# Causal attention core on one core: scores and row maxima in two 64-row tiles of the TensorE array, from two float32r parts, with the causal mask added by products

## What is computed

```python
q = _rope(q, cos, sin)
k = _rope(k, cos, sin)
k = jnp.repeat(k, Q_PER_KV, axis=2)      # 4 query heads share a key head
v = jnp.repeat(v, Q_PER_KV, axis=2)
scores = jnp.einsum('bqhd,bkhd->bhqk', q, k) * SM_SCALE
scores = jnp.where(mask[None, None], scores, jnp.finfo(scores.dtype).min)
probs = jax.nn.softmax(scores, axis=-1)
ctx = jnp.einsum('bhqk,bkhd->bqhd', probs, v).reshape(B, S, HIDDEN)
out = jnp.einsum('bsh,oh->bso', ctx, w_dense) + b_dense
```

## Time and profile before

| what | us |
|---|---|
| time, median of 3 runs (1273.64 to 1277.37) | 1274.57 |
| the profiled execution | 1276.3 |
| its span in the trace | 1274.5 |
| core block: from the projection's last DVE instruction to the first maxima product | 8.77 |
| core block: maxima of group 0 | 29.01 |
| group 0 | 31.10 |
| groups 1 to 6, each | 31.45 |
| group 7 | 28.80 |

### The profile page before, as it was taken

How to read it: one execution, slowest core, us unless ns; L and a number is a source line. 1 busy time by engine, 2 the same in 40 slices (tenths; PEclk the granted TensorE clock), 3 DMA queues, 4 the chain that set the end, 5 groups by cost and what they waited for, 6 DMA issues and landing times. The chain is left out here.

```text
span 1274.5 us, 21579 instructions
## 1 busy us (share of the span) xinstructions
PE 1097.4 (86%) x5654; PEld 717.9 (56%) x5655; DVE 905.9 (71%) x1775; ACT 704.8 (55%) x1218; POOL 566.7 (44%) x582
## 2 busy tenths in 40 slices
PE   4969999999194899999997787999999947878597
PEld 3847777777182233333333675677777735467454
DVE  5869888887575888888860666888888847444632
ACT  3238787887143177777775131787888824424142
POOL 4335666664556244443331225566666545140200
PEclk9979999999596599999998888999999977989889
DMA  9367899764615550000000183789995561000001
GB/s 351 114 220 185 218 243 286 174 114 60 192 50 155 104 99 19 1 1 1 1 1 1 63 309 111 236 196 258 275 222 103 83 156 67 1 1 1 0 1 66
DMA packets 62798, 151.01 MB, mean 118 GB/s; under 512 B 12224, under 2 KB 17024, under 8 KB 58240
## 3 DMA queue, kind: packets, MB, share of 16 engines
q1 hardware_dynamic: 37440, 95.17, 22.3%
q0 software_dynamic: 22592, 50.27, 20.3%
q10 hardware_dynamic: 2688, 4.65, 1.1%
HBM read 104.89 MB, written 44.97 MB: 118 GB/s over the span
## 5 line engine op out<-in xcount | busy, mean ns | idle before, releaser
L811 POOL DMA_INDIRECT moe_acc_rows<-xn,moe_token_of x94 | 208.0, 2213 | 146.3 <-ACT xn L886 131.1
L923 DVE TENSOR_TENSOR moe_w_lo<-moe_raw,moe_w_hi 128x1536 fp32r<-128x1536 f32 x94 | 165.4, 1759 | 62.9 <-ACT moe_w_hi L874 62.7
L1977 ACT ACTIVATE causal_prob<-causal_sc 128x512 f32<-128x512 f32 (+3 forms) x384 | 166.8, 492 | 70.3 <-PE causal_sc L1882 69.7
L874 ACT CAST moe_w_hi<-moe_raw 128x1536 fp32r x94 | 138.7, 1475 | 78.0 <-issue 76.4
L1864 PE MATMUL causal_mx<-ks,causal_qs 96*128 (+4 forms) x384 | 131.4, 353 | 23.0 <-DMA causal_qs<-causal_parts 16.5
L831 PE MATMUL moe_gu<-moe_w_hi,xt_hi 128*128 128x512 f32 x282 | 148.4, 526 | 0.6 <-DVE moe_w_lo L923 0.6
L1882 PE MATMUL causal_sc<-causal_qs,ks 99*128 (+3 forms) x384 | 120.2, 333 | 1.9 <-ACT causal_prob L1977 1.7
L831 PE MATMUL moe_gu<-moe_w_hi,xt_lo 128*128 128x512 f32 x282 | 111.8, 396 | 0.0
L831 PE MATMUL moe_gu<-moe_w_lo,xt_hi 128*128 128x512 f32 x282 | 110.9, 393 | 0.0
L826 PE MATMUL moe_gu<-moe_raw,xn 128*128 x188 | 98.0, 603 | 5.0 <-ACT moe_w_hi L874 5.0
L1808 POOL TENSOR_SCALAR_AFFINE_SELECT causal_prob<-causal_prob 128x512 f32<-128x512 f32 x64 | 40.9, 639 | 115.9 <-ACT causal_prob L1977 115.5
(11 more groups left out here) (317 smaller groups left out, 2724.5 us busy)
## 6 DMA issues: line engine op xcount, KB each, us to landing
moe_raw<-in_w_gu SPq DMA_DIRECT2D x34, 1024.0 KB, 6.1
moe_raw<-in_w_down SPq DMA_DIRECT2D x34, 512.0 KB, 8.2
causal_qs<-causal_parts SPq DMA_DIRECT2D x45, 128.0 KB, 3.6
moe_acc_rows<-moe_zeros SPq DMA_DIRECT2D x2, 2304.0 KB, 14.7
moe_acc_rows<-x SPq DMA_DIRECT2D x18, 256.0 KB, 2.0
moe_xn_rows<-xn SPq DMA_DIRECT2D x2, 2048.0 KB, 10.7
x<-moe_acc_rows SPq DMA_DIRECT2D x16, 256.0 KB, 6.8
xn<-moe_acc_rows ACTq DMA_DIRECT2D x16, 256.0 KB, 7.2
```

Of the source, the lines that this page charges most:

```text
L811: pool.indirect_dma_start(acc_rows[a], bass.IndirectOffsetOnAxis(ap=token_of[:, b - 3:b - 2].bitcast(U32), axis=0), out_rows[(b - 3) % OUT ...
L874: nc.scalar.copy(w_hi[1 - s][:, :, :], raw[:, bass.ds(at + SPLIT_AT, GU_COLS - SPLIT_AT)].rearrange("p (k n) -> p k n", k=SPLIT)).then_inc ...
L923: nc.vector.tensor_tensor(w_lo[1 - s][:, :, :], raw[:, bass.ds(at + SPLIT_AT, GU_COLS - SPLIT_AT)].rearrange("p (k n) -> p k n", k=SPLIT), ...
L1977: nc.scalar.activation(prob[u % 2][:, h, o:CH], sc[(u * QPK + h) % BANKS][:, o:CH], ACT.Exp, scale=SCALE).then_inc(exp_done, 1)
```

## The change

- The parts are two float32r numbers instead of three bfloat16 ones. ACT casts the first, POOL subtracts the second; ACT's second cast and DVE's `third` are gone. DRAM holds 2 parts of 4 bytes.
- A stack is 3 products of 16 rows. There are two copies of it: rows 0 to 49 for scores (with 2 rows for the maxima), rows 64 to 111 for maxima. A score product and a maximum product thus lie in different halves of the array.
- A diagonal maximum is followed by two bfloat16 products of rows 64 to 127, 128 and 64 columns wide, that add the mask: identity by `later`, in two halves of 64 rows.
- DVE reads all maxima with TENSOR_REDUCE; one more instruction per group (`later_best`) joins the two halves for the later 512 queries.
- `split_maxima` has 3 POOL instructions, `put_maxima` 2 DMAs. `turn_maxima` transposes float32.
- Keys and queries have two slots (g % 2) instead of all groups. The loads for group 0, and those of the maxima of group 1, are issued in the projection block. In the core block SP loads the scores' stack of g + 1 and the maxima's of g + 2, after waits on `neg_in[1]`, `sc_done` and `mx_done`.
- At the start of the projection block ACT issues two more loads (64 x 2 x 128 each), waits for both, and casts `mask_q` and `mask_k`; the cast of `ident_half` is gone.
- In group 7, from step 1 on, scores use 112 rows (`ALL_ROWS`); POOL zeroes rows 64 to 127 of a key slot for it at the group's start (`upper_zero`).
- PE's loop over groups is written out.

```diff
-    Q_PART = (0, 0, 1, 0, 1, 2)
-    K_PART = (0, 1, 0, 2, 1, 0)
-    STACK = len(Q_PART) * HD
-    MROWS = 3
+    Q_PART = (0, 0, 1)
+    K_PART = (0, 1, 0)
+    MROWS = 2
+    MAX_AT = 2 * HD
+    SCORE_ROWS = slice(0, 3 * HD + MROWS)
+    MAXIMA_ROWS = slice(64, 64 + 3 * HD)
+    MASK_ROWS = slice(64, P)
+    ALL_ROWS = slice(0, 64 + 3 * HD)
+    IN_SCORES = (0, HD, 2 * HD + MROWS)
+    IN_MAXIMA = (64, 64 + HD, 64 + 2 * HD)
...
                         if r == KEYS[-1] + 1:
...
-                            for a in range(len(Q_PART)):
-                                sp.dma_start(ks[a * HD:(a + 1) * HD, 0:S], parts_dram[K_PART[a], 0:HD, :]).then_inc(stack_in, 16)
+                            load_keys(sp, IN_MAXIMA, 0, for_maxima_in)
+                            load_keys(sp, IN_SCORES, 0, for_scores_in)
+                        if r == QUERIES[-1] + 1:
...
+                            load_queries(sp, IN_MAXIMA, 0, for_maxima_in)
+                        if r == len(TURN) - 1:
+                            load_queries(sp, IN_SCORES, 0, for_scores_in)
+                            sp.wait_ge(for_maxima_in, 16 * LOADS)
+                            load_keys(sp, IN_MAXIMA, 1, for_maxima_in)
+                            load_queries(sp, IN_MAXIMA, 1, for_maxima_in)
...
+                    for n, what in enumerate(("identity", "later")):
+                        act.dma_start(mask_raw[MASK_ROWS, n, :, :], m.dram[what].rearrange("(a p) k -> p a k", a=2)).then_inc(mask_in, 16)
                     act.wait_ge(swap_in, 16)
                     nc.scalar.copy(swap[:, :], swap_raw[:, :]).then_inc(swap_done, 1)
-                    nc.scalar.copy(ident[:, :], m.ident[:, :]).then_inc(consts, 1)
+                    act.wait_ge(mask_in, 32)
+                    nc.scalar.copy(mask_q[MASK_ROWS, :, :], mask_raw[MASK_ROWS, 0, :, :]).then_inc(mask_ready, 1)
+                    nc.scalar.copy(mask_k[MASK_ROWS, :, :], mask_raw[MASK_ROWS, 1, :, :]).then_inc(mask_ready, 1)
...
-                    for a in range(0, len(Q_PART), 2):
-                        first_queries(sp, a)
...
+                    sp.wait_ge(ones_done, 3)
+                    for g in range(KV - 1):
+                        sp.wait_ge(neg_in[1], 16 * MROWS * (g + 1))
+                        if g:
+                            sp.wait_ge(sc_done, g * NS * QPK)
+                        load(IN_SCORES, g + 1, for_scores_in)
...
+                        if g + 2 < KV:
+                            sp.wait_ge(mx_done, (g + 1) * NMU)
+                            load(IN_MAXIMA, g + 2, for_maxima_in)
...
-                        nc.tensor.matmul(mx[i % BANKS][:, 0:w], qs[0:STACK, bass.ds(at, P)],
-                                         ks[0:STACK, bass.ds(gn * S + kc * CH, w)], start=True, stop=True).then_inc(mx_done, 1)
+                        last = nc.tensor.matmul(mx[i % BANKS][:, 0:w], q_r[MAXIMA_ROWS, at:at + P], k_r[MAXIMA_ROWS, key:key + w],
+                                                start=True, stop=not diagonal)
+                        if diagonal:
+                            nc.tensor.matmul(mx[i % BANKS][:, w - P:w], mask_q[MASK_ROWS, 0, :], mask_k[MASK_ROWS, 0, :], start=False, stop=False)
+                            last = nc.tensor.matmul(mx[i % BANKS][:, w - P // 2:w], mask_q[MASK_ROWS, 1, :],
+                                                    mask_k[MASK_ROWS, 1, P // 2:P], start=False, stop=True)
+                        last.then_inc(mx_done, 1)
...
-                        nc.tensor.matmul(sc[b][:, o:CH], ks[0:STACK + MROWS, bass.ds(g * S + kb * P, P)],
-                                         qs[0:STACK + MROWS, bass.ds(g * QG + (h * S + c * CH + o), CH - o)],
+                        rows = ALL_ROWS if g == KV - 1 and u else SCORE_ROWS
+                        if g == KV - 1 and u == 1 and h == 0:
+                            pe.wait_ge(upper_zero, 1)
+                        nc.tensor.matmul(sc[b][:, o:CH], k_r[rows, key:key + P], q_r[rows, at + o:at + CH],
                                          start=True, stop=True).then_inc(sc_done, 1)
...
-                        nc.vector.tensor_tensor_reduce(found, found, no_later[:, CH - w:CH], 1.0, least, ALU.add, ALU.max,
-                                                       top[:, t, h:h + 1]).then_inc(mx_read, 1)
+                        nc.vector.tensor_reduce(top[:, kc, t, h:h + 1], mx[i % BANKS][:, 0:w], AX.X, ALU.max).then_inc(mx_read, 1)
```

197 lines of the change are left out of this document (94 added, 103 removed).

## The result

The changed kernel is slower: 1315.72 us, the median of four executions (1298.91 to 1334.95), against 1275.14 for four of the kernel before, 3.2% more. The ratio is 1.027, 95% interval 1.017 to 1.037; executions over 1.5% above the fastest of their kernel count as slow and stay out of the ratios, here that of 1334.95, in experiment 6 one of 1491.0 at a mean clock of 0.724. I had forecast 1261 and a range of 1250 to 1272. Its four executions lie 36 us apart, where those of before lie within 4 us, and they go with TensorE's mean granted clock: 0.912, 0.900, 0.896 and 0.882 for 1298.91, 1313.13, 1318.31 and 1334.95. The profiled execution is the last of these, 58.7 us over the profiled execution of before (spans of 1333.1 and 1274.5).

A forecast was written before the change was run, and what follows sets the result against it. PE, DVE and the diagonal steps' chain were taken as close limits, plus mutual waiting. Terms -9.5, -5.7, -0.5, +1.6 and +0.3 gave -13.8: 1262.5 us from the profiled 1276.3, 1261 against the median; range 1250 to 1272.

The forecast's parts named there:

- The step that failed is 5: Middle groups: lighter PE and DVE save 1.35 us a group, 9.5 us over seven, bounds 0 and 18.
- step 7: Maxima of group 0, at granted clock 0.50: 0.5 us won, between 3 lost and 2 won.
- the chain keeps the groups as they are: Rival, groups: fourth score, exponential and mask set all steps, PE's relief only makes PE wait; 1270.5 us, chance 11%.
- Steps 1 to 4: Groups: full pair about 0.23 us, diagonal masks 0.9 more on PE, DVE about 25.5, POOL about 1 us less per half-group.
- step 3: DVE in a group: fused maximum 0.65 us, plain one about 0.60; busy time from 27.04 to about 25.5.
- Step 6: Edge of projection and core blocks: early query loads start the first maximum 5.7 us sooner, bounds 4 and 7.
- Step 8: Start of the projection: two more loads and a cast on ACT lose 1.6 us, from 0.3 to 3.
- Step 9: Group 7: a memset ahead of POOL's first split loses 0.3 us.
- The two slowest rivals: Maxima tile: each product pays its own weight load, 1291 us, 11%; score and maximum tiles don't stream together, near 1300, 3%.

The follow-up runs named there:

- experiment 6: Kernel before with diagonal masks as one full-height bfloat16 product and plain maxima, without the two tiles and float32r: 1280.98 us, ratio 1.0036.
- Experiments 1 and 2: First: kernel before, score and maximum products half as high, 1434.94 us. Second: changed kernel, group 7's scores reading 50 rows instead of 112, executions 1306.43 to 1339.98 us.
- experiment 10: Changed kernel with ACT's mask casts moved to the projection's end and SP's wait and loads for group 1 into the core block: 1312.96 us, one execution.
- experiment 3: Changed kernel without the two mask products of each diagonal maximum: 1296.70 us, ratio 1.016.
- experiment 5: Changed kernel plus 96 unread float32r products, 512 wide, reading rows 0 to 47 only: 1306.62 us, ratio 1.026.
- experiment 4: Changed kernel plus 96 unread float32r products, 512 wide and 128 rows high: 1318.41 us, ratio 1.033.

## Why the prediction was wrong

**The step that failed is 5**, the middle group. I put 30.1 us against 31.45, and the bounds at 0 and 18 won in all. It was wrong in two ways.

The larger one is missing from the prediction: that the clock in the groups might not stay at 1.00. I read 1.00 for groups of full-height products and carried it to products half as high. I weighed the clock only for group 0's maxima (step 7), where it stood at 0.50 already. Experiments 1 and 2 show that half-height products let it fall with PE fully busy. In the profiled execution the seven groups take 53.6 us more; at full clock they would take 7 x (32.48 - 31.42) = 7.4 more, and the other 46 are the clock. In the execution near the median (experiment 10) they take 36.1 more, and 28 are the clock.

The smaller one is the size at full clock: +1.1 a group instead of -1.35. By its parts: tiles and masks together 32.48; without masks 31.07, so the tiles alone win 0.35 where I gave PE 3.4; the masks, which I put at 0.9 of PE's time, cost the group 1.4 in the half-height tile (experiment 3) and 0.7 at full height with plain maxima (experiment 6). PE's busy time, which I had fall by 1.9, rose from 30.1 to 31.6. That a middle group is held by its chain (score, exponential, mask, values), as the rival "the chain keeps the groups as they are" said, fits this, but no run shortens the chain. I had given that rival 11% and taken the middle between two bounds instead of asking who waits for PE in the steps that count.

**Steps 1 to 4** held in most of their single prices. Pairs 0.23 apart: measured 0.23, but 0.33 for the first pair after a change of tile. The 0.6 that I added for such turning had no row behind it. DVE 25.5: 25.45. POOL 1 us lighter a half-group: 12.0 against 13.9 a group. A diagonal unit of 512 columns I put at 0.39; at full clock they follow each other every 0.42 where they stream, and in the diagonal steps mostly every 0.60, at DVE's pace (its plain maximum, 0.60 by step 3). On the rule of the Trainium skill that I weighed there ("TensorE: Matmul & The Clock Gate", Part 3, weight loads overlapping only across row groups) the 0.42 speaks against bare weights on all three products, as my did.

**Step 6**, the edge: 5.7 forecast, 1.9 measured (64.91 against 66.85 us from the first `hi_tile` to the first maximum). The core block starts at 410.28, past the 406 that I had named as a sign of being wrong. I took SP's last issue for what is late next and left out what SP waits for behind it, the landing of writes that are queued behind the loads I had moved. POOL's memsets took 6.2 (0.94 + 3.50 + 1.80), as put.

**Step 7**: 0.5 won forecast, 3.5 lost measured (32.53 against 29.01). The mechanism was in the text with both sizes; the clock stayed at 0.50, a unit costs 0.76 against my 0.75, and PE leads DVE. I chose the wrong branch.

**Step 8**: 1.6 forecast, 4.0 measured, over my bound of 3. The second mask load landed 2.2 us behind the swap cast, the casts took 0.7, and the swap matrix itself landed 10.4 after its issue instead of 9.2.

**Step 9**: 0.3 forecast, 2.3 measured. The clock of 0.94 is not all of it: in experiment 5 group 7 ran at 1.00 and took 30.22, as long as here, though with 12 products more; in experiment 4, with 12 full-height ones more, it took 28.99, still 1.2 over the 27.82 of before. The cause stays open.

The two slowest rivals had the right side for reasons that did not hold: tiles do stream together and weights are not bare. My range covered none of it, because no case in it had the clock as its cause.

## What to carry to other kernels

Before halving the height of products that fill PE, ask what the granted clock will do: here the same columns in half the rows took a group from 31.4 to 53.3 us with the engine fully busy, and two such tiles side by side were not enough to hold 2.4 GHz reliably. A relief of the busiest engine is worth what the rest of the stage lets through, here 0.35 us of 3.4. Added full-height products nobody reads cost 1.9 us a group at full clock, and the kernel as a whole came out the same within its spread, with executions 5 us apart instead of 36. A load moved ahead of a write in one queue delays whoever waits for the write: the core block started at 408.85 with the loads ahead of the last writes and at 404.27 with them behind.

## What was not expected of the hardware

The granted clock fell from 1.00 to 0.50 while PE was 90 to 100% busy in every 5 us and its waits in the 15 us before added up to 0.3 at most. It stayed at 0.50 for a whole core block, with PE busy 53.05 of 53.29 us, when products read 48 rows. It made the changed kernel's executions differ by 36 us, in step with the mean clock of 0.912 to 0.882, where those of the kernel before differ by 4. A semaphore wait of 2.8 us in a full-height kernel was followed by about 7 us at 0.50. And queries of 128 KB a load landed at nearly the same time whether issued from 400.4 or from 403.4 on: the maximum that waits for them starts at 409.03 and at 409.92.
